# A decoder layer on one core: small transposes of the side work move to stand right behind an attend

## What is computed

```python
x = x + _L0_attn_ref(_layernorm(x), ...)     # 16 heads of 16, position bias -|i-j| * 0.5**head
x = x + _L0_xattn_ref(_layernorm(x), ctx_1024, ...)  # one head of 256, 77 context rows
x = x + _L0_ffn_ref(_layernorm(x), ...)      # router, top 2 of 8 experts, 256 -> 1024 -> 256, relu
return x
```

## Time and profile before

| | us |
|---|---|
| median of 3 runs | 1608.83 (1608.35 to 1609.33) |
| span of the profiled execution, first to last instruction | 1607.6 |
| PE busy in the span | 1552.3 (97%) |
| DVE busy | 1189.6 (74%) |
| ACT busy | 934.6 (58%) |
| first score of group 1, of group 15 | 152.73, 1036.98 |

### The profile page before, as it was taken

The page is one execution under the profiler, slowest core; times in us unless marked ns, Lnnn a source line. Parts: engine busy times, 40 slices in busy tenths (PEclk is TensorE's granted clock), DMA queues, the critical chain, the costliest instruction groups (busy, mean ns, idle before and its releaser), DMA issues.

```text
span 1607.6 us, 31234 instructions
## 1 busy us (share of the span) xinstructions
PE 1552.3 (97%) x10542; PEld 963.5 (60%) x10542; DVE 1189.6 (74%) x2409; ACT 934.6 (58%) x1786; POOL 387.4 (24%) x462
## 2 busy tenths in 40 slices
PE   5899999999999999999999999999999999999997
PEld 3433443344554444445434443439999999999997
DVE  5888878888877788787877777713354788888885
ACT  3156656677556767664765756772222466666663
POOL 6201120002110041210013100142134334344443
PEclk9799999999999999999999999999999999999998
DMA  6561351232151450314414333234556666766763
GB/s 181 110 126 24 74 122 23 23 43 34 38 99 52 70 86 13 44 41 83 70 51 73 44 106 132 68 130 128 158 179 204 190 199 198 208 191 199 210 192 102
DMA packets 92672, 173.41 MB, mean 108 GB/s; under 512 B 13236, under 2 KB 51124, under 8 KB 92385
## 3 DMA queue, kind: packets, MB, share of 16 engines
q1 hardware_dynamic: 75376, 143.69, 35.2%
q0 software_dynamic: 15744, 26.54, 7.6%
q10 hardware_dynamic: 1392, 1.18, 0.4%
HBM read 133.69 MB, written 37.29 MB: 106 GB/s over the span
## 4 chain that ended last, share of the span: by engine, by line
PE 90%; DVE 4%; ACT 2%; issue 2%; DMA 1%; POOL 0%; SPq 0%; ACTq 0%; DVEq 0%; POOLq 0%
PE ps L1395 16%; PE ps L1183 15%; PE ps L1209 14%; PE ps L1169 13%; PE ps L1138 8%; PE ps L1421 5%; PE ps L1281 2%; PE ps L1315 2%; PE ps L1212 2%; DVE rmax L1632 2%; PE ps L1172 2%; ACT prob L1439 1%; PE ps L1228 1%; PE ps L1383 1%; PE ps L1296 1%
## 5 line engine op out<-in xcount | busy, mean ns | idle before, releaser
L1632 DVE TENSOR_REDUCE rmax<-ps 128x1 f32<-128x512 f32 x960 | 621.2, 685 | 175.4 <-PE ps L1212 86.4
L1439 ACT ACTIVATE prob<-ps 128x512 f32<-128x512 f32 x1024 | 560.8, 601 | 308.2 <-PE ps L1169 157.7
L1209 PE MATMUL ps<-stacked_k,stacked_q 112*128 112x512 bf16 x1024 | 392.1, 390 | 11.4 <-DVE rmax L1629 3.8
L1169 PE MATMUL ps<-stacked_q,stacked_k 115*128 115x512 bf16 x1024 | 358.7, 381 | 3.0 <-ACT prob L1439 1.6
L1183 PE MATMUL ps<-prob,values 128*32 128x512 f32 x2048 | 273.6, 606 | 6.8 <-ACT prob L1439 6.8
L1395 PE MATMUL ps<-xiT,w_now 128*128 128x128 f32 x2272 | 267.5, 275 | 0.0
L1209 PEld LDWEIGHTS ps<-stacked_k,stacked_q 112*128 112x128 bf16 x1024 | 99.5, 99 | 279.2 <-DVE rmax L1632 184.2
L1395 PEld LDWEIGHTS ps<-xiT,w_now 128*128 128x128 f32 x2272 | 262.7, 192 | 1.3
L1169 PEld LDWEIGHTS ps<-stacked_q,stacked_k 115*128 115x128 bf16 x1024 | 97.7, 98 | 152.1 <-ACT prob L1439 67.9
L2060 POOL DMA_INDIRECT out<-yo,xi x71 | 114.9, 1618 | 244.6 <-DVE yo L1935 219.8
L1559 ACT ACTIVATE hidT<-ps,b 128x128 f32<-128x128 f32 x284 | 80.1, 364 | 97.0 <-PE ps L1395 97.0
(11 more groups left out here) (222 smaller groups left out, 1954.7 us busy)
## 6 DMA issues: line engine op xcount, KB each, us to landing
w_now<-in_w SPq DMA_DIRECT2D x71, 1024.0 KB, 5.3
stacked_q<-parts_of_rows SPq DMA_DIRECT2D x90, 128.0 KB, 6.1
stacked_k<-parts_of_rows SPq DMA_DIRECT2D x90, 128.0 KB, 6.7
xi<-expert_rows SPq DMA_DIRECT2D x71, 130.0 KB, 2.2
w<-in_w SPq DMA_DIRECT2D x8, 1024.0 KB, 9.2
parts_of_rows<-q_part SPq DMA_DIRECT2D x21, 256.0 KB, 6.7
parts_of_rows<-k_part SPq DMA_DIRECT2D x21, 256.0 KB, 7.0
xr<-in_x POOLq DMA_DIRECT2D x4, 1024.0 KB, 9.8
```

The lines of the kernel that those rows point to most:

```text
L1169: m = e.matmul(ps[:, bank, :], ka[i][0:ROWS, hh, kt * P:(kt + 1) * P], qa[i][0:ROWS, hh, ch * BANK:(ch + 1) * BANK], start=True, stop=True)
L1209: m = e.matmul(ps[:, bank, :], qa[i][0:MAX_ROW, hh, qt * P:(qt + 1) * P], ka[i][0:MAX_ROW, hh, kc * BANK:(kc + 1) * BANK], start=True, sto ...
L1439: e.activation(prob[:, u % NPROB, :], ps[:, score_bank(u), :], ACT.Exp).then_inc(sem["exp"], 1)
L1632: e.tensor_reduce(rmax[:, G % 2, hh * NT + qt, kc:kc + 1], ps[:, p.bank("max", *k), :], AX.X, ALU.max).then_inc(sem["maxed"], 1)
```

## The change

Two new conditions, `now["apart"]` (true while the attention loop runs) and `now["attended"]` (true in the slot of an attend, right behind it). The small steps wait in `behind_attend` until they stand right behind an attend; a part of a large step waits until it does not. `step_on(closing)`, `step_on(placing)` and `behind` now all run in the slot of an attend; in the other three slots only `behind` runs. So `av_turn`, `on`, `max_turn` and `nrow` too are written in slots of attends alone, one stage of each in a slot.

```diff
+    def behind_attend():
+        while now["apart"] and not now["attended"]:
+            yield 0
+
     def in_parts(*step):
         for i in range(p.parts(step)):
+            while now["apart"] and now["attended"]:
+                yield 0
             p.add_part(i, *step)
...
                 yield from until("turn", which)
                 yield from room()
+                yield from behind_attend()
                 add("turn", which, b, c, four)
...
         if b:
             yield from room()
+        yield from behind_attend()
         add("x_turn", b, c, four)
...
                 yield from until("p_turn")
                 yield from room()
+                yield from behind_attend()
                 add("p_turn", b, two // 2)
...
-    now["running"] = True
+    now["running"] = now["apart"] = True
...
             flush()
-            step_on(placing)
             step_on(staging)
             step_on(scattering)
...
                         if k_ == NT - 1:
                             closing.append(finish(G, c_))
-                            step_on(closing)
+                        now["attended"] = True
+                        step_on(closing)
+                        step_on(placing)
+                        behind(G // NG)
+                        now["attended"] = False
                     else:
-                        step_on(closing)
                         behind(G // NG)
                     maximum(0)
...
+    now["apart"] = False
     while p.open:
         behind(NB - 1)
```

More of the change, by code:

```diff
@@ L627, in step_on @@
             parts.pop(0)
-    now = {"unit": 0, "ended": 0, "spread": 0, "maxima": 0, "running": False, "late": False}
+    now = {"unit": 0, "ended": 0, "spread": 0, "maxima": 0, "running": False, "late": False, "apart": False, "attended": False}
     placing, closing, staging, emptying, scattering = [], [], [], [], []
```

## The result

The changed kernel takes 1644.6 us (median of 4 runs, 1641.0 to 1645.5) against 1609.1 us of the kernel before on the same chip: ratio 1.022, 95% interval 1.0205 to 1.0234. That is 35.5 us more, 10.6 more than forecast, and inside the range.

A forecast was written before the change was run, and what follows sets the result against it. PE was taken to bound the loop, with DVE nearly full. 1607.6 + 0 (PE's work) + 15 (starving) + 5 (late rows) + 5 (late copies) = 1632.6, with 1.2 for the runs' median 1634 us; range 1610 to 1650.

The forecast's parts named there:

- What bounds: Attention loop, groups 1 to 14: PE bounds with 872 of 883 us busy, but DVE has only 18 us left.
- PE's own work: Small steps behind attends: dearer transposes, 4 us more, set against an unpriced saving bounded at 4; taken as 0.
- still take 0.44: Sign in the changed profile: turns 1.00 to 1.05 us behind an attend's start take 0.44 us, as elsewhere.
- Starving: At attends with steps behind: gap without scores and maxima grows 40 us in all; 15 us comes back, between 6 and 22.
- group 3's ratio: Group 3, no side work: PE lost 1.6 us while DVE starved 10.3, or 0.16; gave starving's low end, 6 us.
- How it scales: Starving priced by step length: gap grows 0.44 us behind 87 steps and 0.11 behind 15; bunched side work adds.
- Late rows: `max_turn` and `nrow` wait for attends: PE waits 4 us in group 1, 1 us together in groups 8, 12, 13.
- Late copies: Four times `av` stands behind the next attend, which then waits 1.2 us each: 5 us (3 to 8).
- Where it grows: Attention loop: groups 4, 5, 8 and 9 grow most.
- Fp32 beside fp32: Rival: turns slide into the attend's exit gap, saving 9 us; attend plus turn under 1.35 us; 1605 or 1600; chance 0.10.
- No change: Rival: up to 40 maxima in hand take all starving, only late steps cost; 1610 us, within 0.2%; chance 0.06.
- DVE becomes the bound: Rival: all 40 us of starving come back, and the stalls with them; 1659 us; chance 0.12.

The follow-up runs named there:

- e9: e3 with the small steps' gate one unit ahead of the attend's slot instead of two units behind: 1610.2 us, ratio 1.0001 against the kernel before.
- e2: e1 with `av` also written at once behind the last attend, 87 small steps still behind attends: 1630.6 us, ratio 1.0117 against the kernel before.
- e7: e2 with `step_on(closing)` back as before the change, so only the side work's 56 transposes stand behind attends: 1632.1 us, ratio 1.0145.
- e10: e7 without the growth of shares: the call in an attend's slot adds nothing; 1629.8 us, ratio 1.012 against the kernel before.
- e4: The kernel before with shares that grow by 4/3 a call and no gate: 1629.4 us, ratio 1.0106.
- e1: The changed kernel with `max_turn` and `nrow` driven from every unit again: 1636.8 us, ratio 1.014 against the kernel before.
- e3: e2 with small steps gated two units behind the attend's slot, large steps in the other three slots, shares growing by 4/3: 1615.2 us, ratio 1.0025.
- e6: The kernel before with `logits` in four parts instead of two: 1606.7 us, ratio 0.9984.
- e5: The changed kernel with `logits` in four parts instead of two: 1639.8 us, ratio 1.0174 against the kernel before.

## Why the prediction was right, point by point

- **What bounds.** Right. DVE had no time to lose at the attends. e9 against e2 shows it best: the same kind of gate and the same work, and 34 us less idle time of DVE where the steps stand one unit off.
- **PE's own work, 0 with 4 either way: the upper end.** Behind an attend four transposes hold PE 0.49 us and elsewhere 0.44; 0.05 x 93 is 5 us (the prediction's 96 attends are 93: 102 steps, 9 of them second ones). The sign "still take 0.44" did not come. The row had it (weight loads of 141 against 98 ns, exposed there), and I balanced it with a saving that no row showed. The Trainium skill ("TensorE: Matmul & The Clock Gate", the table of Fast Weight Load) has no fast load for fp32 weights. By it the term would have been the 4 us, and the trace agrees with that size; that the load is the cause was not tested by itself.
- **Starving, 15 us of 40: right in both.** DVE's idle time grew by 36.8 us. e2 holds this and the dearer turns without the late steps: 20.4 us over e9, some 2 of them by its clock, which leaves about 14 beside the dearer turns. The pricing of the trace leaves 13. The nearest row (group 3's ratio, 0.16) was far too low. The middle between 6 and 22 was about right, but no row had chosen it, so that is in part luck.
- **How it scales: partly shown.** I priced each step by its length. By their times e7 and e10, with 56 of 87 steps (0.64), lose as much as e2. By their traces they do not lose it in the same place: outside group 14 the loop grew by 18.8 us in e2, 9.6 in e7 and 12.5 in e10. The part of bunched side work in this term was wrong as a cost of starving: behind a gate off the attend the grown shares cost nothing (e9), without a gate they cost 19 us (e4), by the clock and by PE's waits behind the router's work on DVE. Why e9 has no such waits with the same growth stays open.
- **Late rows, 4 and 1 us: right in group 1 (3.9), nothing in groups 8, 12 and 13.** But e1 gave 7.8 us back; the clock fell in that wait, and what followed ran at half clock.
- **Late copies, 5 us: right.** 4.8 us in four waits; e2 gave 6.2 back, with a fall of the clock in it.
- **The step that was missing: the clock.** The sum took it as granted in full, as in the earlier trace rows. 35.5 less the forecast 24.9 leaves 10.6 us. The mean clock, 0.9842 against 0.9895, is 17 us more at half clock and some 7 us of time by the line above; the pricing of the trace gives 12. With the 3 to 5 us of the dearer turns that covers the miss; starving (13 to 14 us) and the late rows of groups 8, 12 and 13 (nothing) stayed 2 to 3 us under their terms. A rival with that mechanism was not on the list.
- **Where it grows: wrong.** Groups 4, 5, 8 and 9 were to grow most. They grew by 4.3, -1.2, 4.4 and -0.6 us (first score to first score). Groups 11, 0 and 7 grew most, by 8.7, 7.1 and 5.5 us: 0 has the late rows, 7 and 11 have the falls of the clock.
- **The rivals.** "Fp32 beside fp32" fell: attend and turn together took 1.49 us, not under 1.35, and the place directly ahead was no worse. "No change" fell, and "DVE becomes the bound" took more than there was: 27 us of order in place of 50.

## What to carry to other kernels

Where one long instruction group already leaves the other engines dry, do not put more beside it, ahead or behind: one unit ahead of it the same steps were free (e9), two behind it they cost 0.25% (e3). A small fp32 step between bf16 steps took its 0.44 us and nothing more here, so there was nothing to gain by gathering them. If a planner moves steps into rarer slots, look at what each one releases: a copy or a chain of DMAs that comes four units later can meet its reader. And look at the other engines' queues: where small operations gather in front of a reduce, the engine that waits for its bank pays for them.

## What the runs showed of the hardware that I had not expected

TensorE's clock fell to half (1.2 GHz) where the profile shows the engine without a gap. In the 14 profiles the loop has 36 falls. 27 of them begin in or right behind `logits`, fp32 matmuls of 8 columns each; in the kernel before behind 4 us that show PE busy for 4.08 of 4.10 us. Not every `logits` brings one: with two pieces it was 23 of 33. Busy does not mean streaming here. A piece of the changed kernel, weight loads and matmuls:

```profile
832.81 1.86 PEld L1339 LDWEIGHTS ps<-wr,xT 128*128 128x128 f32 x16 [0.31 <-ACT xT L1477]
832.81 1.95 PE L1339 MATMUL ps<-wr,xT 128*128 128x8 f32 x16
```

Its 16 matmuls take 0.11 us each, as long as an fp32 transpose of 128 columns (0.44 us for four), and weight loads fill that time. Whether the few columns, the type or the loads matter, no run separates. Pieces of half the size with bf16 matmuls between them kept the clock at 1.00 in e6, but not in group 11 of e5.

The Trainium skill ("TensorE: Matmul & The Clock Gate", "Why this matters for your kernels") asks for no idle gaps between bursts of matmuls. The other nine falls do follow waits, of 1.3 to 3.9 us (those at 157, 587 and 856 us in the changed kernel waits of 3.9, 1.8 and 1.8 us), but those behind `logits` follow no gap that the profile shows. A us at half clock cost 0.4 to 0.5 us of time.
